# Order of the changeover from tile 0 to group f=1: copies of P1 and P5 moved ahead, rows of B moved back, second half's result behind P3

## The reference

```python
# layer 0
x = x + (einsum('bsi,oi->bso', x, W) + b
         + einsum('bsi,bio->bso', x, 2*mask - 1) * coeff[:, None, None])
# layer 1
def lora_add(base, inp, A, B):
    t = einsum('bri,bni->bnr', A[idx], inp)
    return base + einsum('bor,bnr->bno', B[idx], t) * 0.5
gate = lora_add(x @ W_gate.T, x, A_gate, B_gate)
up   = lora_add(x @ W_up.T,   x, A_up,   B_up)
act  = silu(gate) * up
x = x + lora_add(act @ W_down.T, act, A_down, B_down)
```

## Time and profile before

| | |
|---|---|
| median of 3 runs | 1599.0 us (1595.74, 1599.0, 1599.19) |
| profiled execution | 1594.07 us, span 1592.4 us |
| mean granted clock of TensorE | 0.995 |
| VectorE busy | 1221.5 us (77%) |
| ScalarE busy | 804.6 us (51%) |
| POOL busy | 427.1 us (27%) |
| DMA over the span | mean 205 GB/s |

### The profile page before, as it was taken

One profiled execution on the slowest core, in us unless ns is written; L12 is line 12 of the kernel. 1 busy time (PEld: TensorE's weight loads), 2 busy tenths in 40 slices (PEclk: granted clock), 3 DMA queues, 4 the chain that ended last, 5 costly groups with the idle time before them and its releaser, 6 DMA issues.

```text
span 1592.4 us, 23426 instructions
## 1 busy us (share of the span) xinstructions
PE 1549.6 (97%) x7550; PEld 1305.7 (82%) x7550; DVE 1221.5 (77%) x2136; ACT 804.6 (51%) x1478; POOL 427.1 (27%) x821
## 2 busy tenths in 40 slices
PE   6999998999999999999999979999999999999999
PEld 6999976888888888878888858888888888778887
DVE  8999877766677677688888886677767666788886
ACT  8999855444444444443334464444444444433332
POOL 0000133333333333253410024322313233543100
PEclk9999999999999999999999999999999999999999
DMA  9999853444444444698593625444444445996653
GB/s 373 373 365 368 300 176 114 145 151 146 144 144 156 155 156 155 231 358 268 174 374 111 238 70 174 138 140 139 155 144 149 136 155 181 340 340 208 223 195 118
DMA packets 141962, 325.66 MB, mean 205 GB/s; under 512 B 22417, under 2 KB 50321, under 8 KB 141841
## 3 DMA queue, kind: packets, MB, share of 16 engines
q0 software_dynamic: 61216, 176.21, 32.9%
q1 hardware_dynamic: 76016, 139.57, 25.9%
q10 hardware_dynamic: 4608, 8.39, 1.4%
HBM read 233.51 MB, written 90.18 MB: 203 GB/s over the span
## 4 chain that ended last, share of the span: by engine, by line
PE 86%; DVE 8%; issue 2%; ACT 2%; DMA 1%; SPq 1%; POOL 0%; DVEq 0%; POOLq 0%; ACTq 0%
PE ps L1474 58%; PE ps L1470 25%; PE ps L1612 3%; DVE m_raw L1110 1%; DVE m_lo L1107 1%; DVE acc L1110 1%; DVE lo L1107 1%; DVE op_b L1107 1%; DMA m_raw<-in_mask 1%; DVE raw L1107 1%; DVE fx L1107 0%; DMA b_in<-in_b_gu 0%; DMA x_scratch<-x_out 0%; SPq L504 0%; POOL b_in L644 0%
## 5 line engine op out<-in xcount | busy, mean ns | idle before, releaser
L1474 PE MATMUL ps<-op_b,hi 128*128 128x512 f32 x1616 | 501.6, 392 | 7.1 <-ACT p5c L779 3.7
L1107 DVE TENSOR_TENSOR lo<-raw,hi 128x512 fp32r<-128x512 f32 (+2 forms) x640 | 333.8, 531 | 132.7 <-ACT hi L779 130.7
L779 ACT ACTIVATE hi<-raw 128x512 fp32r<-128x512 f32 (+1 forms) x592 | 305.7, 520 | 222.3 <-PE ps L1474 185.5
L1474 PEld LDWEIGHTS ps<-op_b,hi 128*128 128x128 f32 x1616 | 305.2, 189 | 71.8 <-ACT p5c L779 4.7
L1474 PE MATMUL ps<-op_b,lo 128*128 128x512 f32 x808 | 317.0, 392 | 0.0
L1474 PE MATMUL ps<-op_d,hi 128*128 128x512 f32 x800 | 248.6, 392 | 8.5 <-DVE acc L1110 8.3
L1470 PE MATMUL ps<-op_b,hi 128*128 128x512 f32 x816 | 253.5, 392 | 0.0
L626 POOL DMA_DIRECT2D operand_scratch<-ot x140 | 75.3, 540 | 548.5 <-DVE ot L1107 534.6
L1110 DVE TENSOR_TENSOR acc<-acc,ps 128x512 f32<-128x512 f32 x248 | 170.0, 686 | 53.8 <-PE ps L1474 47.3
L1474 PEld LDWEIGHTS ps<-op_d,hi 128*128 128x128 f32 x800 | 147.9, 188 | 44.3 <-DVE acc L1110 13.9
L1470 PEld LDWEIGHTS ps<-op_b,hi 128*128 128x128 f32 x816 | 154.2, 189 | 31.3
(11 more groups left out here) (130 smaller groups left out, 2323.9 us busy)
## 6 DMA issues: line engine op xcount, KB each, us to landing
operand_scratch<-ot POOLq DMA_DIRECT2D x140, 512.0 KB, 3.9
op_d<-operand_scratch POOLq DMA_DIRECT2D x140, 512.0 KB, 10.6
raw<-in_wgu SPq DMA_DIRECT2D x168, 256.0 KB, 3.9
m_raw<-in_mask SPq DMA_DIRECT2D x64, 512.0 KB, 5.4
raw<-in_wd SPq DMA_DIRECT2D x160, 128.0 KB, 3.8
w_in<-in_w SPq DMA_DIRECT2D x32, 512.0 KB, 6.3
x_scratch<-x_out POOLq DMA_DIRECT2D x32, 256.0 KB, 4.5
acc<-x_scratch POOLq DMA_DIRECT2D x16, 512.0 KB, 6.6
```

The source lines that it names most:

```text
L779: return nc.scalar.activation(o, i, ACT.Copy)
L1107: return nc.vector.tensor_tensor(o, a, b, ALU.subtract)
L1474: return mm(dst, weight, v, start=False, stop=stop, skip_group_check=True)
```

## The change

TensorE's order: "r" 1 moves from behind P7 to directly behind P3. In `first_tile_steps`: the rows of B of f = 0 move from "ta 0,7" to "ta 1,3", behind the adapter weights (1,6); "make4" 2 and 3 (without forming T4) stand at "h 1,5" where 0 and 1 stood; T4's other parts, make4 0 and 1 and all four forms, move behind P6; the mask of half 1 ("t own") moves behind the copy of P1; T3 2 and 3 and the rows of B of f = 1 move behind the copy of P5, which now waits for the making of T4 3 (it has the memory of T2 3) and no longer for T4's forming. The last operand formed is now T4, not T3, and the waits of the second result follow that. The counts of `silu_made` and `a_made` are adapted to the new order.

```diff
-LATER = [(name, k) for name in ("b12", "b22", "t1", "t2", "t4", "t3") for k in range(KQ)]
-MADE = [(name, k) for k in range(KQ) for name in ("t3", "t2", "t1")] + [("t4", k) for k in range(KQ)]
+LATER = [(name, k) for name in ("b12", "b22", "t1", "t2", "t3", "t4") for k in range(KQ)]
+MADE = [(name, k) for k in range(KQ) for name in ("t3", "t2", "t1")] + [("t4", k) for k in (2, 3, 0, 1)]
...
-            ("ta", 0, 7): a_part(1, 2) + [("lora_b", 0), ("t sum", 0), ("make", 3)] + forms("t1", 2)
+            ("ta", 0, 7): a_part(1, 2) + [("t sum", 0), ("make", 3)] + forms("t1", 2)
                           + [("t own", 0), ("t high", 0), ("t low", 0)] + forms("t1", 3),
             ("ta", 1, 1): a_part(1, 4) + forms("t2", 0, 1, 2, 3),
-            ("ta", 1, 3): a_part(1, 6),
-            ("h", 1, 5): [("make4", 0), ("make4", 1)] + forms("t4", 0),
+            ("ta", 1, 3): a_part(1, 6) + [("lora_b", 0)],
+            ("h", 1, 5): [("make4", 2), ("make4", 3)],
             ("r", 0): [("result", 0)],
-            ("h", 1, 6): [("make4", 2), ("make4", 3)] + forms("t4", 1, 2, 3),
-            ("ta", 1, 7): [("t sum", 1)] + forms("t3", 0) + [("t own", 1)],
-            ("g", 1, "p1"): [("t high", 1), ("t low", 1)] + forms("t3", 1, 2) + [("lora_b", 1)] + forms("t3", 3),
+            ("ta", 1, 7): [("t sum", 1)] + forms("t3", 0),
+            ("g", 1, "p1"): [("t own", 1), ("t high", 1), ("t low", 1)] + forms("t3", 1),
+            ("g", 1, "p5"): [("lora_b", 1)] + forms("t3", 2, 3),
+            ("g", 1, "p6"): [("make4", 0), ("make4", 1)] + forms("t4", 0, 1, 2, 3),
             ("r", 1): [("result", 1), ("t neg",)]}
...
-        order += [("g", s, 1, u) for u in PRODUCTS[:5]] + [("r", s, 1), ("g", s, 1, "p2"), ("td", s, 0), ("g", s, 1, "p4")]
+        order += [("g", s, 1, u) for u in PRODUCTS[:4]] + [("r", s, 1)] + [("g", s, 1, u) for u in ("p7", "p2")]
+        order += [("td", s, 0), ("g", s, 1, "p4")]
...
             def first_result(s, half):
                 act.wait_ge(pe_done, done["r", s, half])
                 nc.scalar.activation(g1[:, :], first_bank(0, half)[:, :], ACT.Silu).then_inc(silu_made, 1)
-                act.wait_ge(form_l, form_count(s, *(("t3", KQ - 1) if half else ("t1", 1))))
+                act.wait_ge(form_l, form_count(s, *(("t4", KQ - 1) if half else ("t1", 1))))
...
                 elif u == "p5":
                     if f > 1:
                         act.wait_ge(c_made, c_count(s, f - 1, "c22"))
                     else:
-                        act.wait_ge(form_l, form_count(s, "t4", KQ - 1))
+                        act.wait_ge(form_t, made_count(s, "t4", KQ - 1))
...
             def first_result(s, half):
                 if half:
-                    dve.wait_ge(form_l, form_count(s, "t3", KQ - 1))
+                    dve.wait_ge(form_l, form_count(s, "t4", KQ - 1))
                 dve.wait_ge(pe_done, done["r", s, half])
```

More of the change, by code:

```diff
@@ L365, in silu_count, with a_count @@
         def silu_count(s, f, half):
-            turn = {(0, 1): 3, (1, 1): 2}.get((f, half), 2 * f + (1 + half if f in (0, PAIRS) else 2 - half))
-            return s * (PAIRS * 2 + 2) + turn
-        a_count = silu_count
+            if f < 2 and half:
+                return s * (PAIRS * 2 + 2) + 3 - f
+            return a_count(s, f, half)
+        def a_count(s, f, half):
+            return s * (PAIRS * 2 + 2) + 2 * f + (1 + half if f in (0, PAIRS) else 2 - half)
         def d_count(s, seg, hp, u):
```

## The result

| | before | after |
|---|---|---|
| median of 11 runs each | 1597.26 us (1594.6 to 1599.19) | 1600.92 us (1599.51 to 1602.59) |
| ratio | | 1.0023, 95% interval 1.0014 to 1.0031 |
| profiled execution | 1594.07 us, span 1592.4 | 1600.95 us, span 1599.3 |
| mean granted clock | 0.995 | 0.989 |

The change makes the kernel slower by 0.23%, some 3.7 us. The forecast was 1601.1 us, 2.1 slower: the range holds the time, the sign is right and the forecast loss is a little over half of the measured one.

A forecast was written before the change was run, and what follows sets the result against it. TensorE, busy 97%, was held by changeover waits on VectorE's and ScalarE's queues, plus low clock. Losses of 0.9 us in block 0 and 1.2 in block 1, 2.1 in all, on the 1599.0 median gave 1601.1 us; range 1594.5 to 1605.5.

The forecast's parts named there:

- The sum behind the rows of B: VectorE, tile 0: sum 1.1 us earlier in block 0, 0.7 to 0.8 in block 1; lw(1,4) wait 1.25 instead of 2.45.
- the 0.16 that a modelled end hides: TensorE's printed waits: each starts at a modelled end 0.39 us after the last start, not 0.23, so costs 0.16 more.
- The wait ahead of r 0: TensorE, each block: r 0 waits 4.7 us for rows of B made behind lw(1,6), replacing 0.68 at (1,6).
- Copies of P1 and P5: Changeover: earlier copies end P6's wait (2.63 us saved in block 0, 1.0 in block 1); P3 waits 0.5.
- T4's parts ahead of P3's sum: VectorE behind P6: six ops, 3.6 us; P3's sum starts at 255.5, not 254.13; td 0's wait grows from 2.36 to 4.5.
- u2 behind the result: VectorE: four result ops ahead of u2, which P4 needs; P4 waits another 1.6 us, previously nothing.
- the 1 to 2 named as a sign: Sign of a right forecast: TensorE waits 1 to 2 us ahead of P4 for u2.
- The clock: Low clock after both new waits: +1.6 us behind r 0, +0.8 behind td 0 per block; chance 0.52.
- the sign that went with it: Sign of a right forecast: granted clock near 0.7 after the wait ahead of r 0.
- The clock didn't stay high: First rival: clock stays high after the new waits; 2.7 us faster, 1596.3; chance 0.18.
- the second rival: Clock stays low longer than 3.5 us after each 4.7 us wait: 8.5 us slower, 1607.5; with half, 1604; chance 0.25.
- The B rows do hold r 0: Third rival claimed the opposite: r 0 not held, saving up to 4.7 us per block, time 1587; chance 0.05.

The follow-up runs named there:

- an order with shorter waits: Changed kernel with the rows of B directly behind lw(1,4) and T4's parts back in tile 0: 1586.49 us, ratio 0.9937 to the kernel before.

## Why the prediction was right, point by point

That 1600.92 us came out for a forecast of 1601.1 is luck in part: the forecast stands on the median of three runs, 1599.0, which is 1.7 us above the median of eleven, and its loss of 2.1 us is 1.6 too small. What holds is the order of the waits, their releasers and most of their sizes.

**1. The sum behind the rows of B** was forecast 1.1 us earlier; it ran at 220.06 instead of 221.74, with block 0 0.27 us early, so 1.4 earlier. lw(1,4)'s wait was to be 1.25 us and was 1.12 + 0.16 (the 0.16 that a modelled end hides, as in the prediction). Right, a little better than forecast.

**2. The wait ahead of r 0**: 4.7 us forecast, 4.69 + 0.16 and 4.65 + 0.16 measured, with the releaser named. Right, and all three profiles have it. Taken alone on the kernel before it costs nothing in the end (ratio 0.9998): the 4.7 us replace waits that the same queues cause before and behind it. In the changed kernel, with those removed, undoing it gives 0.4%.

**3. Copies of P1 and P5**: no wait ahead of P6, 0.31 + 0.16 ahead of P3 for a forecast of 0.5. Right. The load of T4 3 and the rows of B of f = 1 made no wait.

**4. T4's parts ahead of P3's sum**: forecast at 255.5 at full clock, measured 257.80. Of the 2.3 us, P1's late start by the clock behind r 0 gives most. The wait ahead of td 0 was to be 4.5 and was 4.33 + 0.16. The run with T4's parts back shows that this is the step that loses most.

**5. u2 behind the result**: 1.6 us forecast ahead of P4, 0.45 + 0.16 measured, less than the 1 to 2 named as a sign, since td 0's own slow matmuls took up 1.0 of it; the forecast had taken 0.8. With the clock kept up by unused matmuls it is 1.35 (and 1.33 with T4's parts back).

**The clock** is the term that was mis-sized, and the sign that went with it: the granted clock was to be near 0.7 behind r 0 and was 0.52 from 233 to 239 in block 0 (0.72 from 930.7 to 936.7 in block 1). Behind r 0 in block 0, 13 matmuls take 5.62 us from 233.23 to 238.85 for some 3.1, a loss of 2.5 us where 1.6 was taken; in block 1 4.69 for 3.1, 1.6 as forecast. After td 0 the forecast let 0.8 us through; P4's 14 matmuls alone take 5.32 us (265.13 to 270.45) for 3.3 in block 0 and 5.09 in block 1, so 2.0 and 1.8 us got through. With these 0.9 + 0.9 + 1.2 is 3.0 us for block 0 (2.60 measured) and 1.2 + 1.0 is 2.2 for block 1 (2.10 measured). The 1.2 us per down product stood nowhere in the sum, and no run ties them to the change.

**The rivals.** The clock didn't stay high. It stayed low longer than the usual length in part, which is the second rival at a part of its price. The B rows do hold r 0. The Trainium skill, "TensorE: Matmul & The Clock Gate", section "HAM oscillation — how this bites in real kernels", has the rule that a stall between matmuls can send the array to the lower clock. The traces agree for the long waits: in all three profiles of the changed kernel, both waits of each block were followed by low clock.

All fourteen profiles of this case together give a plainer picture than the prediction had. A wait of a changeover counts as followed by low clock here where the matmuls from it to the next wait, or the first 16 of them, take 0.9 us or more longer than at full clock. Of 17 waits of 1.3 to 1.8 us, one was followed by low clock (ahead of P4, block 1, with T4's parts back); of 21 waits of 2.1 to 2.7 us, 14; of 31 waits of 2.9 us and more, all.

**The base.** That 3.7 us came out and not the 4.7 of the two changeovers is within what the timed runs scatter; it can't be booked to a step. The upper end of the range is called half way into the second rival, which would be 1604.3 and not 1605.5; the result is under both.

## What to carry to other kernels

A step that is moved in an in-order queue has two prices: who needs it first (r 0, ahead of the place it was moved to) and what stands behind it now (P3's sum, behind T4's six ops). So before a block of side work is moved, look whether its old place was a hole: here it was one (3 us of idle VectorE), and the new place was on the path. A wait of TensorE also has a second price, the low clock behind it: here it cost 1.6 to 2.5 us after a wait of 4.7, about 1.6 after most waits of 2.1 to 2.7, and nothing after 16 of the 17 waits of 1.3 to 1.8. So cutting a long wait in two only pays if the pieces are short: with the 4.7 us wait alone on the kernel before, in place of several shorter ones, the time was the same (0.9998). Dead matmuls in the long waits gave the clock back here, but an order with shorter waits gave twice as much (0.9937 against 0.9982, from 1.0023).

## What the hardware showed beyond expectation

Filling two waits of 4.7 and 4.3 us per block with unused matmuls gave 0.4% with no step moved, and the granted clock over both stretches went from 0.52 and 0.57 to 1.00. After a wait of 4.7 us the loss was 2.5 us in one block and 1.6 in the other of the same execution. The wait of 2.3 us at the start of the down product was followed by low clock in all three executions of one kernel and in neither of the two executions of another, though it is the same wait at the same distance from the changeover (418.2 us before, 418.2 after); this stays open.
